# Masked graph attention on one core: one of four row tiles of the middle stage's mask transposed by VectorE

## The reference

```
h   = relu(layernorm(x))                       # 8192 x 256
h1  = h @ a[:256];  h2 = h @ a[256:]           # one number for each row
e   = leaky_relu(h1 + h2.T, 0.01)              # 8192 x 8192
att = softmax(where(adj > 0, e, -9e15), axis=1)
out = x + att @ h
```

## Time and profile before

| what | value |
|---|---|
| median of 3 runs | 1551.02 us (1548.48 to 1551.06) |
| the profiled execution | 1552.08 us, of which the span from the first to the last instruction is 1550.3 us |
| busy: TensorE matmul | 1522.7 us (98%) |
| busy: VectorE | 1489.6 us (96%) |
| busy: ScalarE | 1162.5 us (75%) |
| busy: GpSimd | 457.4 us (30%) |
| mean granted TensorE clock | 0.999 of full speed |

### The profile page before, as it was taken

One profiled execution on the slowest core, in us unless ns is written; L12 is line 12 of the kernel. 1 busy time (PEld: TensorE's weight loads), 2 busy tenths in 40 slices (PEclk: granted clock), 3 DMA queues, 4 the chain that ended last, 5 costly groups with the idle time before them and its releaser, 6 DMA issues.

```text
span 1550.3 us, 38852 instructions
## 1 busy us (share of the span) xinstructions
PE 1522.7 (98%) x12678; PEld 1511.9 (98%) x12678; DVE 1489.6 (96%) x2172; ACT 1162.5 (75%) x1180; POOL 457.4 (30%) x547
## 2 busy tenths in 40 slices
PE   5999999999999999999999999999999999999999
PEld 5999999999999999999999999999999999999998
DVE  7999999999999999999999999999999999999998
ACT  7787877778777777677776876777777777677774
POOL 6363334335452340120420320320320320420420
PEclk9999999999999999999999999999999999999999
DMA  6666677787778799999999999999999999999994
GB/s 211 222 200 230 206 223 227 230 248 221 245 220 254 220 225 233 221 201 206 218 207 207 224 204 207 226 197 210 230 195 205 228 195 207 217 195 209 219 199 98
DMA packets 436493, 331.05 MB, mean 214 GB/s; under 512 B 16704, under 2 KB 378176, under 8 KB 436416
## 3 DMA queue, kind: packets, MB, share of 16 engines
q1 hardware_dynamic: 411360, 288.94, 83.6%
q10 hardware_dynamic: 25056, 41.13, 8.7%
HBM read 308.90 MB, written 21.10 MB: 213 GB/s over the span
## 4 chain that ended last, share of the span: by engine, by line
PE 82%; DMA 5%; DVE 3%; ACT 3%; issue 2%; SPq 1%; ACTq 0%; DVEq 0%
PE acc L950 27%; PE acc L953 26%; PE acc L952 26%; DMA adj_in<-in_adj_dram 5%; PE T L917 2%; ACT mask L542 2%; DVE w_lo L797 1%; DVE halves L786 1%; SPq L268 1%; ACT w_hi L552 0%; DVE T L767 0%; DVE w_lo L801 0%; ACT w_hi L555 0%; DVE adj_in L901 0%; DVE adj_in L896 0%
## 5 line engine op out<-in xcount | busy, mean ns | idle before, releaser
L950 PE MATMUL acc<-h_hi,w_hi 128*128 128x258 f32 (+1 forms) x4096 | 1167.3, 285 | 9.2 <-DVE w_lo L801 3.4
L953 PE MATMUL acc<-h_hi,w_lo 128*128 128x258 f32 (+1 forms) x4096 | 1153.3, 282 | 0.0
L952 PE MATMUL acc<-h_lo,w_hi 128*128 128x256 f32 (+1 forms) x4096 | 1149.7, 281 | 0.0
L950 PEld LDWEIGHTS acc<-h_hi,w_hi 128*128 128x128 f32 x4096 | 771.8, 188 | 17.8 <-issue 8.0
L952 PEld LDWEIGHTS acc<-h_lo,w_hi 128*128 128x128 f32 x4096 | 778.4, 190 | 0.1
L953 PEld LDWEIGHTS acc<-h_hi,w_lo 128*128 128x128 f32 x4096 | 775.3, 189 | 0.0
L786 DVE SCALAR_TENSOR_TENSOR halves<-r_rep,g_all,T 128x512 f32<-128x512 f32 (+1 forms) x1024 | 712.7, 736 | 10.8 <-PE T L917 1.5
L542 ACT ACTIVATE mask<-adj_in,mhalf 128x2048 fp8e5<-128x2048 int32 x256 | 510.3, 1993 | 58.8 <-DMA adj_in<-in_adj_dram 58.5
L552 ACT ACTIVATE w_hi<-halves 128x1024 fp32r<-128x1024 f32 x336 | 353.6, 1057 | 185.0 <-DVE halves L786 172.3
L797 DVE SCALAR_TENSOR_TENSOR w_lo<-halves,w_hi 128x1024 fp32r<-128x1024 f32 x336 | 418.2, 1245 | 9.9 <-PE acc L953 4.9
L555 ACT ACTIVATE w_hi<-halves 128x1024 fp32r<-128x1024 f32 x176 | 185.3, 1057 | 97.5 <-DVE halves L786 92.6
(11 more groups left out here) (70 smaller groups left out, 343.8 us busy)
## 6 DMA issues: line engine op xcount, KB each, us to landing
adj_in<-in_adj_dram SPq DMA_DIRECT2D x672, 256.0 KB, 5.0
adj_in<-in_adj_dram SPq DMA_DIRECT2D x88, 1024.0 KB, 6.3
part_sums<-stage ACTq DMA_DIRECT2D x24, 516.0 KB, 5.6
xo<-part_sums ACTq DMA_DIRECT2D x24, 516.0 KB, 4.4
r_rep<-r_rows SPq DMA_DIRECT2D x39, 256.0 KB, 4.8
xb<-in_x_dram ACTq DMA_DIRECT2D x15, 512.0 KB, 5.9
out_dram<-xb ACTq DMA_DIRECT2D x15, 512.0 KB, 4.7
xb<-in_x_dram SPq DMA_DIRECT2D x14, 512.0 KB, 5.8
```

The lines of the kernel that those rows point to most:

```text
L950: nc.tensor.matmul(acc[:, t, 0:WC], w_hi[:, k % HL, cols], rhs_hi, start=start and u == 0, stop=False)
L952: nc.tensor.matmul(acc[:, t, 0:D], w_hi[:, k % HL, cols], rhs_lo, start=False, stop=False)
L953: last = nc.tensor.matmul(acc[:, t, 0:WC], w_lo[:, k % LL, cols], rhs_hi, start=False, stop=stop and u == 1)
```

## The change

`MID` goes from 0 to 1: in visits 6 to 21 the fourth row tile of each chunk's mask is transposed by VectorE and the other three by TensorE. `N_MID` becomes 12, the first iteration of visit 6. VectorE's transposition for `dt` between 0 and 4 is placed at odd steps, for the chunk that comes next: behind `subtract(g - 2)` and ahead of the side work and of `weights(g)`, which are the second weights of the chunk in front of it. It waits for `s_T` of its chunk. With `dt = 4` it stays where it was.

```diff
-    MID, LATE = 0, 4
-    N_MID = 2 * 22
+    MID, LATE = 1, 4
+    N_MID = 2 * 6
...
                 if dt:
                     act.wait_ge(s_turn[kc], 64 * (n - N_MID + 1))
-                if dt == G and not (isinstance(n, int) and n == N_MID):
+                if dt == G:
                     act.wait_ge(s_TV, (n - N_MID) * CI + kc - 1)
...
-            def transpose_mask(V, n, kc):
+            def transpose_mask(n, kc, dt):
 
                 g = n * CI + kc
-                t = G - V.dt
-                if V.dt < G:
+                t = G - dt
+                if dt < G:
                     dve.wait_ge(s_T, g + 1)
                 else:
                     dve.wait_ge(s_mask, g + 1)
...
-                        if V.dt and k % 2 == 0:
-                            transpose_mask(V, n, kc)
+                        if V.dt == G and k % 2 == 0:
+                            transpose_mask(n, kc, G)
                         if not (isinstance(V.v, int) and V.v == 1 and first and k < 2):
                             subtract(g - 2, (k + 2) % 4, True, V.deep and not (enter and k < 2))
+                        dt = V.dt_next if last and kc == 1 else V.dt
+                        if 0 < dt < G and k % 2 == 1:
+                            transpose_mask(n + (kc + 1) // CI, (kc + 1) % CI, dt)
                         if first:
                             side_work(V, k)
```

## The result

| | before | after |
|---|---|---|
| median | 1549.99 us (4 runs) | 1592.97 us (1590.27 to 1594.45, 4 runs) |
| ratio | | 1.0268, 95% interval 1.0252 to 1.0284 |
| span of the profiled execution | 1550.3 us | 1590.3 us |

The kernel became 2.7% slower. The forecast was 1594 us. A ratio is estimated by itself and is not exactly the quotient of the two medians.

What follows compares the result with a forecast made beforehand. TensorE was taken as the stage's bound, kept full by VectorE's lead. Path 17.9, side work 15.6, evacuation 5.0 and GpSimd 4.0 summed to 42.5 us, giving 1594 us, 2.7% slower, range 1568 to 1616.

Steps and rivals of the forecast that it cites:

- The bound of the stage: Visits 6 to 21: TensorE, busy all 391 us, is the bound; VectorE's lead of 1.8 us keeps it full.
- The path: From TensorE's transposes through VectorE's transposition, weights and subtraction to the products: chunk 6.43 us instead of 6.15, 17.9 us in all.
- Side work: Stats and scores at odd steps, between transposition and weights, fall inside the path: 15.6 us.
- Evacuation: At visit starts TensorE's first product waits for ScalarE's first accumulator copy: 0.31 us in 16 visits, 5.0 us.
- GpSimd: A subtraction slowed beside L399, 1.79 us instead of 1.22, reaches the path once in each of 7 early visits: 4.0 us.
- TensorE's 5.8 us: One transpose of 0.09 us taken from TensorE in each of 64 chunks, all gained if nothing else happened.
- Rival 1: VectorE's lead covers the wait and the time falls by TensorE's 5.8 us to 1545; chance 4%.
- rival 2: The path fits without side work, so only side work and evacuation show, less some TensorE gain: 1569; chance 12%.
- rival 6: Gain and stalls cancel, leaving a result within 0.2%; chance 2%.
- Rival 3: Small load pieces land late, a quarter of 64 at 1.4 us adding 22 us: 1616; chance 8%.
- rival 4: VectorE's short transposition costs nearly what the long one does, 0.40 us more in each chunk: 1619; chance 5%.
- rival 5: TensorE's clock falls because it idles each chunk, one fall per visit adding 37 us: 1631; chance 4%.

Runs made afterwards that it cites:

- The wait alone: Kernel before plus only VectorE's wait for the next chunk's T at odd steps of the same 64 chunks: 1583.48 us, ratio 1.0205.
- early-only kernel: Changed kernel, VectorE transposing one row tile at its own chunk's first step only in visits 7 to 19 (early ones) and 21: 1552.95 us, ratio 1.0005.
- own-step kernel: Changed kernel with the transposition at its own chunk's even step, behind that step's subtraction and ahead of its first weights: 1553.45 us, ratio 1.0007.
- the loads alone: Changed kernel's loads, all four row tiles transposed by TensorE and none by VectorE in this stage: 1552.43 us, ratio 1.0001.

## Why the prediction was right, step by step

The mechanism was the one forecast. That the sum, 42.5 us, met the 43.0 measured so closely is in part luck: the term of the path was too small by 2 us, and those of the evacuation and of GpSimd were too large by 1 and by nearly 2 us.

**The bound of the stage.** That TensorE set the time through VectorE's lead, and not VectorE through its total work, is shown by the three places of one instruction: 1593 us ahead of the side work and the weights, 1577 behind the side work, 1552 behind the weights, with the work of every engine unchanged. The wait alone gives 1583.

**The path.** By its parts, forecast and measured in the chunk shown, from the start of the transposes: VectorE starts at 0.62 (0.65), weights at 0.84 (0.89), the subtraction at 2.16 (2.17), its end at 3.38 (3.39), the products at 3.48 (3.54), the next chunk at 6.43 (6.46). The transposition of 128 columns took 0.24 us from its start to the next instruction, for which 0.22 was worked out from wider instructions. 64 x (6.46 - 6.15) = 20 us, where 17.9 was forecast.

**Side work.** The next chunk, with scores at its odd step, lasts 364.11 - 356.94 = 7.17 us:

```profile
361.18 0.36 PE L953 MATMUL acc<-h_hi,w_hi 128*128 128x258 f32 x1 [0.91 <-ACT w_hi L555]
...
364.11 0.49 PE L920 MATMUL T<-ident,mask 128*128 128x128 f32 x3
```

Here too the record names the next step's rounding; the subtraction that these products need ended at 361.03. The chunk is 0.71 longer than one without side work at its odd step, for a forecast 0.68. The term as a whole was 15.6 us, and moving the transposition behind the side work gave back 16.

**Evacuation.** In a late visit the first product starts 3.75 us after the transposes (forecast 3.79), behind the first copy:

```profile
343.77 0.49 PE L920 MATMUL T<-ident,mask 128*128 128x128 f32 x3
...
347.52 0.39 PE L953 MATMUL acc<-h_hi,w_hi 128*128 128x258 f32 x1 [0.40 <-ACT stage L574]
```

The chunk lasts 350.48 - 343.77 = 6.71 us, 0.25 over the others, and the trace has this wait once in each of the 16 visits: 4 us, for a forecast 5.0. In two late visits this chunk was longer still, 7.09 and 6.84 us, which stays unexplained. That this stall has no other cause was argued from the rows; no run took it away by itself.

**GpSimd.** Here a size and the place were off. The forecast took 0.57 us for a subtraction beside L399 in each early visit, 4.0 us. In the early visit that begins near 371 us L399 runs from 385.55 to 389.34, and the subtraction inside it, at 387.46, lasts 1.30 us in place of 1.22. Its chunk takes 6.54 us, 0.08 over 6.46, and in all seven early visits with `stats` it takes 6.51 to 6.55: 0.5 us together. But in the same visits the first chunk has its subtraction beside L390, another GpSimd line, which the forecast had not looked at:

```profile
373.81 1.50 DVE L801 SCALAR_TENSOR_TENSOR w_lo<-halves,w_hi 128x1024 fp32r<-128x1024 f32 x1
```

Five such chunks, with 1.50 to 1.51 us, take 7.22 to 7.24 us, and two with 1.37 us take 7.06 and 7.08. By the other terms each would take 7.04, so that is 1 us more in all. Visit 21 has no `stats` and was not in the term, and it has both: subtractions of 1.70 us beside L390 and 1.69 us beside L399, with chunks 0.34 and 0.47 us too long. Together GpSimd cost some 2.3 us for a forecast 4.0. With 19.8 us of the path, 16 of side work and 4 of evacuation this makes 42.1 us of the 42.5 by which the stage grew. That the longer subtractions made these chunks longer is read from the rows; no run took GpSimd's work away.

**TensorE's 5.8 us.** They are inside the 6.46. Off the path they appear in most chunks (6.03 to 6.09 us), but are lost where VectorE falls behind. The prediction's arithmetic of spare time (23 us against 14) is right for the stage and says too much: the spare time is not there in every chunk. In the stretch of eight chunks VectorE had 49.25 - 46.20 = 3.05 us, of which the transpositions took 1.8. Where it falls behind can be read in three traces: at the subtraction beside L399 in the last chunk of an early visit, in the early-only kernel as in the own-step kernel and the one behind the weights, and in the last two also behind the scores.

**The rivals.** Rival 1 (VectorE's lead covers the wait) and rival 2 (the path fits without side work) fall with the 6.46 us chunk, rival 6 (gain and stalls cancel) with the ratio. Rival 3 (late loads) falls with the loads alone, rival 4 (a dear short instruction) with 0.24 us, rival 5 (the clock) with the granted 1.00 over a stage with one idle gap in nearly every chunk.

**The rest of the span.** From the last group's last transpose to the end there were 988.8 us before and 986.3 after, 2.5 us less. This is no gain of the change: the same stretch, in which all kernels here do the same, took 984.6 us with the transposition behind the weights and 993.1 in the own-step kernel. With one trace for each kernel this is no proof, but it is where single executions seem to scatter: in those two kernels the stage itself took 388.3 and 387.8 us.

## What to carry to other kernels

A wait in an in-order queue costs what stands behind it, not what it waits for: before adding one, compare the time at which it can end with the latest time at which each instruction behind it may start, and put it behind those that are urgent. An engine's lead over its consumer is the thing to read from the timeline (here 1.8 us); busy shares showed 6% to spare, and the lead was gone all the same. Where a wait can't be moved, put work that nobody waits for ahead of it.

## What the runs showed that I had not expected

The subtraction beside GpSimd's L399 lasted 1.79 us in one execution and 1.30 us in another kernel's, with GpSimd's instructions equally long (3.80 and 3.79 us for four). The rows of single instructions show what decides. First the kernel before, whose subtraction starts at 315.67, then the kernel after:

```profile
315.65 0.73 POOL L399 TENSOR_TENSOR h_lo<-halves,h_hi 128x256 f32 x1
```

```profile
386.94 0.73 POOL L399 TENSOR_TENSOR h_lo<-halves,h_hi 128x256 f32 x1
387.46 1.30 DVE L801 SCALAR_TENSOR_TENSOR w_lo<-halves,w_hi 128x1024 fp32r<-128x1024 f32 x1
```

What counts is how much of the GpSimd instruction under way is left when the subtraction starts: 0.71 us in the first case and 0.21 in the second. The subtraction lasted that plus 1.08 us, and never less than the 1.21 to 1.22 that it takes alone. Counted over the stage in the ten traces of this case, there are 303 subtractions that start while a GpSimd TENSOR_TENSOR of some 0.74 us is under way (L390, L399 or L410, in the line numbers of the kernel before), and 299 of them keep to this within 0.02 us. In the other four a second whole GpSimd instruction ran inside the subtraction, which lasted 0.62 us longer. So moving the start of an instruction by half a microsecond, as the wait did here, can change its length by as much.
